# A cross-attention and FFN kernel: the out-projection four tiles ahead of the FFN in the last stage, and the residual loaded into the place of tiles 12 and 13

## The chip, the cores and the metric

The kernel runs on one core of a Trainium2 chip. The metric is the device time in microseconds (us) of one execution; lower is better. The engines are PE (TensorE, matrix products), DVE (VectorE), ACT (ScalarE), POOL (GpSimd) and SP (SyncE, which here only issues DMAs). Each works through its own list of instructions in order, and they meet through semaphores.

## The reference

Eight batch entries of 1024 tokens attend to 2048 context tokens each, with 16 heads of 32, and then pass through a linear layer whose input and weight are quantised in blocks of 32. Both halves add to the residual. Width is 512 throughout.

```python
def xattn(x, context, mask, Wq, Wk, Wv, Wo, bo, g1, b1, g2, b2):
    xn, cn = layer_norm(x, g1, b1), layer_norm(context, g2, b2)
    q, k, v = heads(xn @ Wq.T), heads(cn @ Wk.T), heads(cn @ Wv.T)
    scores = einsum('bqhs,bkhs->bhqk', q, k) / sqrt(32)
    attn = softmax(where(mask, scores, -inf))
    return einsum('bhqk,bkhs->bqhs', attn, v).reshape(B, Tx, C) @ Wo.T + bo

def ffn(x, weight, bias):            # both operands: blocks of 32, scale = max|block| / 7.5,
    xq, xs = mx_quantize(x)          # values rounded to the nearest of a 6-bit grid
    wq, ws = mx_quantize(weight)
    return (xq * xs) @ (wq * ws).T + bias

x = x + xattn(layernorm(x), ctx_1024, mask, ...)
x = x + ffn(layernorm(x), weight, bias)
```

## The kernel before

The kernel is written engine by engine: every engine has one block of code, an outer loop over the eight batch entries `b`, and the order of its instructions is the order in which the code is written. Nothing schedules them afterwards. A `wait_ge(semaphore, count)` holds everything behind it on the same engine.

**Stages of a batch.** `front()` turns and projects the tokens (queries, keys, values, in split half precision). Then eight units (`unit`, four head groups times two halves of the queries) make scores, exponentials and weighted sums in steps over 16 context tiles. Exponentials of a context tile lie in one of four buffers `PR[0]` to `PR[3]`, the four quarters of the big buffer `region` (`R`); POOL adds them in pairs (`pair`, L399) into `SUMS`, and DMAs that add on landing merge these (`merge`, L410). After the last unit comes the last stage, which the change is about.

**The last stage.** It works on 8 tiles of 128 tokens. For tile i:

- PE makes the out-projection, `contract(bank(i % 2), ...)` at L858 with `WO` (woT): four matmuls in float32 that the trace shows as eight passes. It waits for `s_x1`, that is for DVE to have emptied the bank two tiles before.
- POOL has added the bias `bo_all` to the residual `X1[:, i, :]` (`out_bias`, L456). `X1` lies in `R[:, 0:4096]`, the same memory as `PR[0]` and `PR[1]`.
- DVE adds bank and residual (`x1_tile`, L667), takes mean and variance (L498, L503, L510).
- POOL makes the inverse deviation (`x1_rstd`, L463, L465), and ACT writes the normalised tile to `XD` (L818).
- DVE quantises (`quantise`, L531 to L540), and POOL multiplies back to full size into `XD` (`full_size`, L470). POOL also adds the FFN bias `wb_all` to `X1` (L483).
- PE turns `XD` (four transposes, `turn`, L833) into bank 2 or 3, ACT copies it to `XDT` (L814), and PE makes the FFN contraction with `WD` (wdT) into bank 4 or 5 (again L858). `WD` doubles as `SUMS[4]` in the attention and is loaded again for each batch.
- DVE adds it to `X1` (`y_tile`, L685), and SP stores the tile.

On PE the step i of the loop is: out-projection i, turn i-2, FFN contraction i-2. DVE's step i is: quantise i-1, add i, FFN addition i-3, then a piece of the norm of the next batch's first tokens (`parts`, L498, L513). ACT's is: copy of turn i-2, normalise i. In the last two steps PE also turns the next batch's first tokens (`first_turns`, into banks 6 and 7), which ACT copies with an affine step (L718) and POOL subtracts (`low_tokens`, L380); the next batch's first projection pass (L864) waits for the last of these.

Bank 6 (`OB`) holds the weighted sums of a unit, bank 7 (`LB`) its row sums. Before the stage ACT copies bank 6 (L780), and in its first microsecond bank 7 (L760). DVE inverts the row sums (L601) and multiplies the outputs of the last unit (L608); out-projections 4 to 7 wait for that (`s_an`).

On SP the loads of the stage stand in this order behind the bias rows `bo` and `wb`: the FFN weights, the residual in two halves, the next batch's first tokens in two chunks, the projection weights. The first one waits for the last weighted step.

Of the kernel before, what the change touches and what calls it, by code (L numbers as in the profile page):

```python
# [8 lines left out]
P = 128  # L9
# [39 lines left out]
def build(nc, x, ctx_in, mask, wqT, wkT, wvT, woT, bo, affine_in, w, wb, out):  # L49
# [7 lines left out]
    KT = C // P  # L57
# [48 lines left out]
    with ExitStack() as es:  # L106
# [53 lines left out]
        PJB = [OB, LB]  # L160
        TURN = PS[0:J * QT, 4, 0:P]
# [77 lines left out]
        def _(e):  # L239
# [39 lines left out]
            for b in range(0, B):  # L279
# [45 lines left out]

                e.wait_ge(s_pv, b * (NU * KT) + NU * KT + 4)
                e.dma_start(SUMS[4], wd_dram).then_inc(s_fl, 16)
                for h in range(2):
                    e.dma_start(X1[:, 4 * h:4 * h + 4, :], xb[:, h]).then_inc(s_xl[h], 16)
# [163 lines left out]
        def _(e):  # L493
# [76 lines left out]
            for b in range(B):  # L570
# [93 lines left out]
                def x1_tile(i):  # L664
                    e.wait_ge(s_op, b * TT + i + 1)
                    e.wait_ge(s_xb, b * TT + i + 1)
                    e.tensor_tensor(X1[:, i, :], bank(i % 2), X1[:, i, :], ALU.add).then_inc(s_x1, 1)  # L667
# [162 lines left out]
        def _(e):  # L830
# [13 lines left out]
            for b in range(0, B):  # L844
# [212 lines left out]

                first_turns = turn_chunk(b + 1, 0, 6) if b + 1 < B else iter(())
                for i in range(TT + 2):
                    if i % 4 == 0 and i < TT:  # L1060
                        e.wait_ge(s_an, b * NU + NU + i // 4)
                    if i < TT:
                        if i >= 2:
                            e.wait_ge(s_x1, b * TT + i - 1)
                        contract(bank(i % 2), lambda cc: AO[:, ds((2 * cc + i // 4) * AO_UNIT + i % 4 * P, P)],
                                 lambda cc: WO[:, cc, :]).then_inc(s_op, 1)
                    if i >= 2:
                        k = i - 2
                        e.wait_ge(s_xd, 4 + b * TT + k + 1)
                        if k >= 2:  # L1070
                            e.wait_ge(s_tc, 4 + b * TT + k - 1)
                        turn(bank(2 + k % 2), lambda c: XD[k % 2][:, c * P:c * P + P]).then_inc(s_tt, 1)
                        if i >= TT:
                            next(first_turns, None)
                            next(first_turns, None)
                        e.wait_ge(s_tc, 4 + b * TT + k + 1)
                        if k >= 2:
                            e.wait_ge(s_y, b * TT + k - 1)
                        if k == 0:
                            e.wait_ge(s_fl, b * 16 + 16)  # L1080
                        contract(bank(4 + k % 2), lambda cc: XDT[k % 2][:, cc, :],
                                 lambda cc: WD[:, cc, :]).then_inc(s_ff, 1)
# [28 lines left out]
```

## Time and profile before

| | |
|---|---|
| median of 3 runs | 4893.51 us (4892.85 to 4898.69) |
| profiled execution, device time | 4894.66 us |
| its span, first to last instruction | 4892.9 us |
| PE busy | 4593.8 us |
| DVE, ACT, POOL busy | 3379.8, 2838.0, 2971.8 us |
| mean granted TensorE clock | 0.986 of full |

Busy time is the time in which an engine worked on an instruction; the rest of the span it waited. In a timeline each row is one instruction or a merged run of like ones; the number in brackets is how long its engine had been idle before it and what released it. Some rows further down cut the span in stretches; they give the stretch and its length, then for PE, PEld (weight loads), DVE, ACT and POOL the busy time and the number of instructions, then the granted TensorE clock (1.00 is 2.4 GHz, 0.50 is 1.2 GHz), the share of time in which the DMA engines were busy, and GB/s.

### The profile page before, as it was taken

The numbers are of one execution on the slowest core, as the hardware profiler recorded it, in microseconds if no ns is written. First come the engines' busy times: TensorE is split into PE (matmuls) and PEld (weight loads), VectorE is DVE, ScalarE is ACT, GpSimd is POOL, SyncE is SP. The second block draws the span as 40 slices with busy tenths as digits, with TensorE's granted clock in tenths as the row PEclk, the third lists the DMA queues.
The fourth block names the chain that finished last, engine by engine and source line by source line (L and its number), as shares of the span: only waits on it lengthen the run. The fifth ranks groups of instructions, "written<-read, shape, count | busy, mean of one in ns | idle before, by whom it ended". The sixth has DMA issues, their size and how long they took to land.

```text
span 4892.9 us, 65384 instructions
## 1 busy us (share of the span) xinstructions
PE 4593.8 (94%) x24720; PEld 1348.4 (28%) x24720; DVE 3379.8 (69%) x3943; ACT 2838.0 (58%) x5128; POOL 2971.8 (61%) x1818
## 2 busy tenths in 40 slices
PE   4999899998999989999899998999989999899998
PEld 2322242222422224222242222422224222342222
DVE  4788457884588855888357884588855887458873
ACT  3477634775347753477544774457744577446773
POOL 2278743777438773387634876347863578625875
PEclk9999999999999999999999999999999999999999
DMA  5255632555325553355533555335543355443552
GB/s 182 64 118 104 147 113 60 118 111 152 99 65 105 119 147 102 70 104 118 141 102 71 111 110 140 104 72 117 108 134 109 73 116 112 127 113 80 106 119 75
DMA packets 189918, 530.81 MB, mean 108 GB/s; under 512 B 28625, under 2 KB 102673, under 8 KB 148386
## 3 DMA queue, kind: packets, MB, share of 16 engines
q0 software_dynamic: 43776, 318.79, 32.3%
q1 hardware_dynamic: 145826, 207.83, 13.8%
q8 instruction: 195, 3.19, 0.3%
q14 instruction: 121, 0.99, 0.1%
HBM read 110.98 MB, written 21.01 MB: 27 GB/s over the span
## 4 chain that ended last, share of the span: by engine, by line
PE 75%; ACT 10%; DVE 6%; SPq 3%; DMA 3%; issue 2%; POOL 1%; ACTq 0%; DVEq 0%; POOLq 0%
PE banks L957 21%; PE banks L947 19%; PE banks L864 12%; PE banks L923 9%; PE banks L858 7%; ACT region L743 7%; PE banks L983 5%; DVE max_parts L583 3%; SPq L293 3%; PE banks L833 2%; DMA region<-in_x 1%; DVE region L574 1%; ACT values L814 1%; ACT region L718 0%; POOL wkT_wvT_wqT L399 0%
## 5 line engine op out<-in xcount | busy, mean ns | idle before, releaser
L583 DVE TENSOR_REDUCE max_parts<-banks 128x2 f32<-128x1024 f32 x2048 | 2400.1, 1218 | 469.2 <-PE banks L923 468.2
L743 ACT ACTIVATE region<-banks 128x512 f32<-128x512 f32 x4096 | 2211.0, 596 | 695.9 <-PE banks L947 656.9
L399 POOL TENSOR_TENSOR wkT_wvT_wqT<-region 128x1024 f32<-128x1024 f32 x608 | 1474.7, 2549 | 556.5 <-ACT region L743 554.3
L947 PE MATMUL banks<-queries_stacked,keys_stacked 98*128 98x512 f16 x4096 | 1298.4, 387 | 82.2 <-ACT region L743 50.7
L957 PE MATMUL banks<-region,values 128*32 128x512 f32 x8192 | 1100.6, 609 | 18.5 <-ACT region L743 7.7
L947 PEld LDWEIGHTS banks<-queries_stacked,keys_stacked 98*128 98x128 f16 x4096 | 289.0, 97 | 1438.7 <-ACT region L743 1356.4
L923 PE MATMUL banks<-keys_stacked,queries_stacked 33*128 33x512 f16 x4096 | 658.7, 384 | 7.0 <-DVE max_parts L583 3.5
L864 PE MATMUL banks<-region,wkT_wvT_wqT 128*128 128x512 f16 x2304 | 574.6, 388 | 48.1 <-POOL region L380 23.0
L601 DVE RECIPROCAL row_sums_inverse<-row_sums_inverse 128x128 f32<-128x128 f32 x256 | 232.0, 930 | 437.9 <-ACT row_sums_inverse L760 437.9
L399 POOL TENSOR_TENSOR sums<-region 128x1024 f32<-128x1024 f32 x160 | 395.7, 2631 | 25.7 <-ACT region L743 25.5
L574 DVE SCALAR_TENSOR_TENSOR region<-banks,region 128x512 f16<-128x512 f32 x192 | 132.2, 689 | 346.7 <-ACT region L726 345.7
L864 PE MATMUL banks<-wkT_wvT_wqT,region 128*128 128x512 f16 x1536 | 369.1, 380 | 0.0
L399 POOL TENSOR_TENSOR wdT<-region 128x1024 f32<-128x1024 f32 x128 | 314.4, 2595 | 1.5 <-ACT region L743 0.4
L923 PEld LDWEIGHTS banks<-keys_stacked,queries_stacked 33*128 33x128 f16 x4096 | 159.6, 93 | 559.9 <-issue 298.0
L726 ACT ACTIVATE region<-banks 128x512 f16<-128x512 f32 x192 | 113.7, 597 | 343.0 <-PE banks L864 286.2
L380 POOL TENSOR_TENSOR region<-row_sums_inverse,region 128x512 f16<-128x512 f32 x80 | 92.5, 1156 | 339.9 <-ACT region L718 339.9
L864 PEld LDWEIGHTS banks<-region,wkT_wvT_wqT 128*128 128x128 f16 x2304 | 214.6, 100 | 302.8 <-issue 65.0
L858 PE MATMUL banks<-wdT,values 128*128 128x512 f32 x512 | 249.8, 633 | 48.2 <-ACT values L814 48.2
L730 ACT ACTIVATE values<-banks 128x512 f32<-128x512 f32 x128 | 76.4, 597 | 334.0 <-PE banks L864 334.0
L858 PE MATMUL banks<-woT,queries_stacked 128*128 128x512 f32 x512 | 245.2, 627 | 26.3 <-DVE region L667 26.3
L416 POOL DMA_DIRECT2D wdT<-wkT_wvT_wqT x96 | 99.9, 1040 | 275.9 <-ACT region L743 155.3
L957 PEld LDWEIGHTS banks<-region,values 128*32 128x32 f32 x8192 | 161.6, 108 | 380.7 <-ACT region L743 219.3
(83 smaller groups left out, 2905.3 us busy)
## 6 DMA issues: line engine op xcount, KB each, us to landing
wdT<-wkT_wvT_wqT POOLq DMA_DIRECT2D x96, 1024.0 KB, 11.4
wkT_wvT_wqT<-wkT_wvT_wqT POOLq DMA_DIRECT2D x80, 1024.0 KB, 7.0
sums<-wkT_wvT_wqT POOLq DMA_DIRECT2D x72, 1024.0 KB, 7.0
keys_stacked<-region SPq DMA_DIRECT2D x768, 64.0 KB, 2.0
wkT_wvT_wqT<-sums POOLq DMA_DIRECT2D x40, 1024.0 KB, 7.0
region<-in_x SPq DMA_DIRECT2D x24, 1024.0 KB, 10.0
wkT_wvT_wqT<-weights_split SPq DMA_DIRECT2D x8, 3072.0 KB, 19.3
queries_stacked<-region SPq DMA_DIRECT2D x384, 64.0 KB, 2.0
```

The source lines that it names most:

```text
L293: e.dma_start(dst, KS[HD * j:HD * j + HD, part, gs, :]).then_inc(s_kd[h], 16)
L399: e.tensor_tensor(SUMS[dst][:, half], PR[i][:, half], PR[i + 1][:, half], ALU.add).then_inc(s_pr, 1)
L574: e.scalar_tensor_tensor(KS[:, 1, i, :], PJB[j % 2], 1.0 / W_SCALE, KS[:, 0, i, :], ALU.mult, ALU.subtract).then_inc(s_k2, 1)
L583: e.tensor_reduce(mpart[:, buf, :, a, t, c], MXB[parity], AX.X, ALU.max).then_inc(s_mxd, 1)
L601: inv = e.reciprocal(part, part)
L743: e.activation(PR[u % 4][:, j * HALF:j * HALF + HALF], score_bank(kt, j)[0], ACT.Exp, scale=SCALE).then_inc(s_ex, 1)
L858: mm = e.matmul(bank, lhs(cc), rhs(cc), start=(cc == 0), stop=(cc == CC - 1))
L864: mm = e.matmul(bank, lhs(p, cc), rhs(r, cc), start=(cc == 0 and i == 0), stop=(cc == CC - 1 and i == 2))
L923: mm = e.matmul(MXB[parity][:, i, :], QA[rows, ds(((2 * g + q) * J + 2 * a + i) * HALF + t * P, P)], KA[rows, ds((g * J + 2 * a + i) * C + ...
L947: e.matmul(dst, KA[0:STR, ds(ka + (j * C + (u + 1) * P), P)], QA[0:STR, ds(qa[j], HALF)], start=True, stop=True).then_inc(s_st, 1)
L957: mm = e.matmul(OB[HD * j:HD * j + HD, :], V[:, ds(v + u * D + HD * j, HD)], PR[u][:, j * HALF:j * HALF + HALF], start=False, stop=end, sk ...
L983: mm = e.matmul(LB[HD * j:HD * j + HD, :], ones[:, :], src[:, ds(j * HALF, HALF)], start=False, stop=closing and i == len(sums) - 1, skip_ ...
```

## The change

Three things are done. Line numbers of the changed kernel lie 3 to 6 above those before.

1. PE makes the out-projections of tiles 0 to 3 at once, in banks 0, 1, 6 and 7, and stays four tiles ahead: behind turn k (k below 4) comes out-projection k+4, then FFN contraction k. Tile 2 waits until ACT has copied bank 6, tile 3 until it has copied bank 7, later tiles for DVE's addition four tiles back.
2. From turn 4 on, turn k+1 is issued before FFN contraction k, so that ACT's copy of one turn runs while PE contracts another. The next batch's tokens are turned half before turn 7 and half before FFN contraction 7; since they are written to banks 6 and 7, the first half also waits for DVE's addition of tile 7.
3. SP loads the residual into `X1` before the FFN weights, as soon as the weighted step of context tile 13 of the last unit is done and POOL has added the last pair (context tiles 12 and 13, in `PR[0]` and `PR[1]`).

DVE, ACT and POOL keep their order; DVE only reads tile i from `out_bank(i)`.

```diff
+        LEAD = 4
+        out_bank = lambda i: bank((0, 1, 6, 7)[i % LEAD])
...
+                e.wait_ge(s_pv, b * (NU * KT) + (NU - 1) * KT + 14 + 4)
+                e.wait_ge(s_pr, 14 * (b * NU + NU) + 2)
+                for h in range(2):
+                    e.dma_start(X1[:, 4 * h:4 * h + 4, :], xb[:, h]).then_inc(s_xl[h], 16)
                 e.wait_ge(s_pv, b * (NU * KT) + NU * KT + 4)
                 e.dma_start(SUMS[4], wd_dram).then_inc(s_fl, 16)
-                for h in range(2):
-                    e.dma_start(X1[:, 4 * h:4 * h + 4, :], xb[:, h]).then_inc(s_xl[h], 16)
...
-                    e.tensor_tensor(X1[:, i, :], bank(i % 2), X1[:, i, :], ALU.add).then_inc(s_x1, 1)
+                    e.tensor_tensor(X1[:, i, :], out_bank(i), X1[:, i, :], ALU.add).then_inc(s_x1, 1)
...
+                def out_project(i):
+                    if i % 4 == 0:
+                        e.wait_ge(s_an, b * NU + NU + i // 4)
+                    if i == 2:
+                        e.wait_ge(s_oc, b * NU + NU + 1)
+                    if i == 3:
+                        e.wait_ge(s_on, b * NU + NU + 1)
+                    if i >= LEAD:
+                        e.wait_ge(s_x1, b * TT + i - LEAD + 1)
+                    contract(out_bank(i), ...).then_inc(s_op, 1)
...
-                for i in range(TT + 2):
-                    ...
+                for i in range(LEAD):
+                    out_project(i)
+                for k in range(TT):
+                    if k < LEAD:
+                        turn_quantised(k)
+                        out_project(k + LEAD)
+                    if k == TT - 2:
+                        e.wait_ge(s_x1, b * TT + TT)
+                        next(first_turns, None)
+                        next(first_turns, None)
+                    if LEAD - 1 <= k < TT - 1:
+                        turn_quantised(k + 1)
+                    if k == TT - 1:
+                        next(first_turns, None)
+                        next(first_turns, None)
+                    ffn(k)
```

`turn_quantised(k)` and `ffn(k)` are the old turn and FFN contraction with the waits they had.

PE at the start of the last stage of batch 0, as it was. `woT` rows are the out-projection, `ident,values` the turn of a quantised tile, `wdT` the FFN contraction; a row without x stands for one instruction:

```order
L858 MATMUL banks<-woT,queries_stacked 128x512 [waits unit_normalised]
L858 MATMUL banks<-woT,queries_stacked 128x512 x7
L858 MATMUL banks<-woT,queries_stacked 128x512 [waits x1_made]
L858 MATMUL banks<-woT,queries_stacked 128x512 x3
L833 MATMUL banks<-ident,values 128x128 [waits quantised]
L833 MATMUL banks<-ident,values 128x128 x3
L858 MATMUL banks<-wdT,values 128x512 [waits ffn_weights_loaded,quantised_copied]
L858 MATMUL banks<-wdT,values 128x512 x3
L858 MATMUL banks<-woT,queries_stacked 128x512 [waits x1_made]
L858 MATMUL banks<-woT,queries_stacked 128x512 x3
```

And as it is now:

```order
L864 MATMUL banks<-woT,queries_stacked 128x512 [waits unit_normalised]
L864 MATMUL banks<-woT,queries_stacked 128x512 x7
L864 MATMUL banks<-woT,queries_stacked 128x512 [waits unit_outputs_copied]
L864 MATMUL banks<-woT,queries_stacked 128x512 x3
L864 MATMUL banks<-woT,queries_stacked 128x512 [waits unit_row_sums_copied]
L864 MATMUL banks<-woT,queries_stacked 128x512 x3
L839 MATMUL banks<-ident,values 128x128 [waits quantised]
L839 MATMUL banks<-ident,values 128x128 x3
L864 MATMUL banks<-woT,queries_stacked 128x512 [waits x1_made,unit_normalised]
L864 MATMUL banks<-woT,queries_stacked 128x512 x3
L864 MATMUL banks<-wdT,values 128x512 [waits ffn_weights_loaded,quantised_copied]
L864 MATMUL banks<-wdT,values 128x512 x3
```

The wait for DVE's addition has gone from tile 2, which now waits for ACT's copy of bank 6; the out-projections of tiles 2, 3 and 4 have moved ahead of FFN contraction 0.

PE at the end of the same stage, where `ident,region` are the next batch's first tokens and `region,wkT_wvT_wqT` is its first projection. Before:

```order
L833 MATMUL banks<-ident,values 128x128 [waits quantised_copied,quantised]
L833 MATMUL banks<-ident,values 128x128 x3
L833 MATMUL banks<-ident,region 128x128 [waits tokens_normalised]
L833 MATMUL banks<-ident,region 128x128 x7
L858 MATMUL banks<-wdT,values 128x512 [waits y_made,quantised_copied]
L858 MATMUL banks<-wdT,values 128x512 x3
L833 MATMUL banks<-ident,values 128x128 [waits quantised_copied,quantised]
L833 MATMUL banks<-ident,values 128x128 x3
L833 MATMUL banks<-ident,region 128x128 [waits transposed_copied]
L833 MATMUL banks<-ident,region 128x128 x3
L833 MATMUL banks<-ident,region 128x128 [waits transposed_copied]
L833 MATMUL banks<-ident,region 128x128 x3
```

Now:

```order
L864 MATMUL banks<-wdT,values 128x512 [waits y_made,quantised_copied]
L864 MATMUL banks<-wdT,values 128x512 x3
L839 MATMUL banks<-ident,region 128x128 [waits tokens_normalised,x1_made]
L839 MATMUL banks<-ident,region 128x128 x7
L839 MATMUL banks<-ident,values 128x128 [waits quantised_copied,quantised]
L839 MATMUL banks<-ident,values 128x128 x3
L864 MATMUL banks<-wdT,values 128x512 [waits y_made,quantised_copied]
L864 MATMUL banks<-wdT,values 128x512 x3
L839 MATMUL banks<-ident,region 128x128 [waits transposed_copied]
L839 MATMUL banks<-ident,region 128x128 x3
L839 MATMUL banks<-ident,region 128x128 [waits transposed_copied]
L839 MATMUL banks<-ident,region 128x128 x3
```

FFN contraction 5 stands at the top of the second piece and turn 7 behind the first half of the token turns, where turn 6 stood ahead of them; the second half no longer stands behind turn 7.

SP behind the load of `bo`, before:

```order
L324 DMA values<-in_wb 128x512
L327 DMA wdT<-ffn_weights_quantised 128x2048 [waits pv_steps_done]
L329 DMA region<-in_x 128x4x512 x2
L243 DMA region<-in_x 128x4x512
L243 DMA values<-in_x 128x4x512
L275 DMA wkT_wvT_wqT<-weights_split 128x6144
```

Now:

```order
L327 DMA values<-in_wb 128x512
L333 DMA region<-in_x 128x4x512 [waits exponentials_paired,pv_steps_done]
L333 DMA region<-in_x 128x4x512
L335 DMA wdT<-ffn_weights_quantised 128x2048 [waits pv_steps_done]
L246 DMA region<-in_x 128x4x512
L246 DMA values<-in_x 128x4x512
```

The two halves of the residual moved ahead of the FFN weights, behind a wait of their own.

## Rows read from the trace of the kernel before

**Rows 1.** The page: busy time, share of the span and instructions of each engine.

```profile
PE 4593.8 (94%) x24720; PEld 1348.4 (28%) x24720; DVE 3379.8 (69%) x3943; ACT 2838.0 (58%) x5128; POOL 2971.8 (61%) x1818
```

**Rows 2.** Windows, the last stage of batches 0 and 7; columns as described above.

```profile
595.02:671.73 76.71, 66.10 (x181) 30.38 (x178) 53.05 (x119) 17.13 (x25) 42.80 (x46) 0.96 0.35 134
...
4811.18:4888.36 77.18, 64.58 (x164) 28.63 (x160) 42.32 (x93) 11.77 (x17) 34.52 (x40) 0.96 0.18 65
```

**Rows 3.** Timeline of PE, batch 0: start, duration, line, operation, tiles, [idle before].

```profile
595.02 7.13 PE L858 MATMUL banks<-woT,queries_stacked 128*128 128x512 f32 x16
605.51 5.40 PE L858 MATMUL banks<-woT,queries_stacked 128*128 128x512 f32 x8 [3.36 <-DVE region L667]
...
615.09 5.40 PE L858 MATMUL banks<-wdT,values 128*128 128x512 f32 x8 [2.40 <-ACT values L814]
...
625.05 3.70 PE L858 MATMUL banks<-wdT,values 128*128 128x512 f32 x8 [0.69 <-ACT values L814]
628.59 3.60 PE L858 MATMUL banks<-woT,queries_stacked 128*128 128x512 f32 x8
632.02 0.60 PE L833 MATMUL banks<-ident,values 128*128 128x128 f32 x4
...
666.88 1.04 PE L833 MATMUL banks<-ident,region 128*128 128x128 f32 x8
...
671.73 0.59 PE L864 MATMUL banks<-region,wkT_wvT_wqT 128*128 128x512 f16 x2 [0.29 <-POOL region L380]
```

**Rows 4.** Timeline of DVE, the same stage.

```profile
599.27 0.69 DVE L608 TENSOR_TENSOR queries_stacked<-queries_stacked,row_sums_inverse 128x512 f32<-128x512 f32 x1
604.77 0.69 DVE L667 TENSOR_TENSOR region<-banks,region 128x512 f32<-128x512 f32 x1 [4.81 <-POOL region L456]
...
610.17 0.69 DVE L540 TENSOR_TENSOR row_sums_inverse<-values,inv 128x512 fp8e4<-128x512 f32 x1
610.78 0.68 DVE L667 TENSOR_TENSOR region<-banks,region 128x512 f32<-128x512 f32 x1
...
624.15 0.68 DVE L667 TENSOR_TENSOR region<-banks,region 128x512 f32<-128x512 f32 x1
...
630.66 0.69 DVE L540 TENSOR_TENSOR row_sums_inverse<-values,inv 128x512 fp8e4<-128x512 f32 x1
...
648.73 0.69 DVE L667 TENSOR_TENSOR region<-banks,region 128x512 f32<-128x512 f32 x1 [1.48 <-PE banks L858]
...
655.03 0.69 DVE L540 TENSOR_TENSOR row_sums_inverse<-values,inv 128x512 fp8e4<-128x512 f32 x1
656.99 0.69 DVE L667 TENSOR_TENSOR region<-banks,region 128x512 f32<-128x512 f32 x1 [1.27 <-PE banks L858]
```

**Rows 5.** Timeline of POOL, the same stage.

```profile
603.40 2.48 POOL L456 TENSOR_TENSOR region<-region,values 128x512 f32<-128x512 f32 x2 [16.46 <-DMA region<-in_x]
...
610.94 1.04 POOL L470 TENSOR_TENSOR values<-row_sums_inverse,scale 128x512 f32<-128x512 fp8e4 x1 [1.99 <-DVE row_sums_inverse L540]
...
663.35 1.05 POOL L470 TENSOR_TENSOR values<-row_sums_inverse,scale 128x512 f32<-128x512 fp8e4 x1 [1.76 <-DVE row_sums_inverse L540]
```

**Rows 6.** Timelines of SP and POOL, the loads' landing at L329, the page's DMA issues.

```profile
595.15 0.33 SPq L327 DMA_DIRECT2D wdT<-ffn_weights_quantised  x1
...
581.99 4.95 POOL L399 TENSOR_TENSOR wkT_wvT_wqT<-region 128x1024 f32<-128x1024 f32 x2
...
DMA to landing us min/median/max: 7.6/8.8/10.5
...
sums<-wkT_wvT_wqT POOLq DMA_DIRECT2D x72, 1024.0 KB, 7.0
```

**Rows 7.** Windows: tile 2 of batch 0, then two periods from stage to stage.

```profile
605.51:610.91 5.40, 5.39 (x8) 2.03 (x8) 3.07 (x10) 0.81 (x1) 2.44 (x4) 0.68 1.09 413
...
1800.15:2400.84 600.69, 571.76 (x3093) 167.80 (x3089) 415.79 (x489) 353.59 (x640) 370.69 (x225) 0.99 0.47 108
2400.84:3006.25 605.41, 575.96 (x3093) 167.74 (x3089) 415.65 (x489) 353.38 (x640) 370.71 (x225) 0.98 0.46 108
```

More of the change, by code:

```diff
@@ L1055, in _ @@
                 unit(G - 1, 1, True)
-                first_turns = turn_chunk(b + 1, 0, 6) if b + 1 < B else iter(())
-                for i in range(TT + 2):
[L1060 to L1082, printed above, removed]
@@ new lines, in out_project @@
+                def out_project(i):
[7 more added lines that the diff above has]
+                        e.wait_ge(s_x1, b * TT + i - LEAD + 1)
+                    contract(out_bank(i), lambda cc: AO[:, ds((2 * cc + i // 4) * AO_UNIT + i % 4 * P, P)],
+                             lambda cc: WO[:, cc, :]).then_inc(s_op, 1)
@@ new lines, in turn_quantised, with ffn @@
+                def turn_quantised(k):
+                    e.wait_ge(s_xd, 4 + b * TT + k + 1)
+                    if k >= 2:
+                        e.wait_ge(s_tc, 4 + b * TT + k - 1)
+                    turn(bank(2 + k % 2), lambda c: XD[k % 2][:, c * P:c * P + P]).then_inc(s_tt, 1)
+                def ffn(k):
+                    e.wait_ge(s_tc, 4 + b * TT + k + 1)
+                    if k >= 2:
+                        e.wait_ge(s_y, b * TT + k - 1)
+                    if k == 0:
+                        e.wait_ge(s_fl, b * 16 + 16)
+                    contract(bank(4 + k % 2), lambda cc: XDT[k % 2][:, cc, :],
+                             lambda cc: WD[:, cc, :]).then_inc(s_ff, 1)
```

## Prediction

> **What bounds the kernel now.** I read the page first. PE is busy 94% of the span [rows 1], so a gain has to come from where PE waits or from its clock. The change touches one stage, the last of each of eight batches, so I cut the span by stage: from the first pass of the out-projection to the first projection pass of the next batch it takes 76.71 us in batch 0, with PE busy 66.10 us of it, and in the last batch, up to the end of DVE's last addition, 77.18 us [rows 2]. The other six stages repeat the first within 0.3 us. All times below count from that first pass (595.02 in batch 0).
>
> PE's timeline of the stage shows three parts [rows 3]. First two tiles in 7.13 us, then a wait of 3.36 us for DVE's addition on tile 0 (L667); tile 2 then takes 5.40 us where a later one takes 3.60, and the first FFN contraction, after another wait of 2.40 us, again 5.40. Then a regular loop: FFN contraction (3.70, with a wait of 0.69 before it for ACT's copy), out-projection (3.60), turn (0.60). From start to start the two contractions take 3.54 and 3.43, turn and wait 1.29: 8.26 us a tile. Last, a tail of FFN contractions and turns of the next batch's tokens, whose last one starts 4.85 us before the next batch's first pass (666.88 to 671.73).
>
> Why the first wait: the residual is loaded behind the FFN weights after the last weighted step (queue SP at 595.15), the 16 loads of it land after 7.6 to 10.5 us [rows 6], POOL adds the bias at 603.40 [rows 5], and DVE's first addition starts at 604.77 although DVE was through with the normalising product that starts at 599.27 [rows 4].
>
> The second chain that matters is the one across engines for a tile: DVE adds and takes statistics, POOL makes the deviation, ACT normalises, DVE quantises, and only then adds the next tile. Its rate where PE does not hold it is in [rows 4]: 6.01 us from tile 0 to 1, 13.37 us for the next two (6.69 each). After tile 3 the loop waits for PE, so I rebuild its own rate from DVE's quantising product (L540), behind which an addition can start after 0.61 us (the addition at 610.78 follows such a product at 610.17, and XD is written by POOL until 611.98, 1.20 us after the addition's start [rows 4, 5]). Tile 3 began at 624.15 and its product at 630.66: 7.12 us a tile; tile 4, which also has the next batch's centring in it, repeats that; tile 5, without it, repeats the 6.69; tile 6 runs from 648.73 to 655.03 plus 0.61: 6.91. This chain needs 6.0 to 7.1 us a tile and PE's loop 8.26, so PE's loop sets the pace now.
>
> **Part 1, the residual loaded earlier.** The two loads now stand ahead of the FFN weights, released by the weighted step of tile 13 and POOL's last pair, whose two halves start at 581.99 and take 4.95 us: about 586.95 [rows 6]. Landing is bounded by the present 7.6 to 10.5 us, with other loads on the same queue: 594.6 to 597.5, and sooner for the first half, which alone is wanted. POOL has nothing else then. The bias needs 1.24 us a tile, so tile 0 would be ready by 598.8 at the latest. Then DVE is late next: its product at 599.27 frees it 0.61 us later, so the first addition starts at 599.88, or 4.86, not 9.75. Price of the moved issues: SP waits there with nothing else behind it that is due before 595.15, and the last merge, which POOL issues before those two pairs (before 581.99) and which lands 7.0 us later, by 589.0, overlaps them by some 2 us; PE wants that buffer only in the last passes before 595.02, so about 5 us of slack cover it [rows 3, 6]. FFN weights and the next batch's tokens start no later than before, with 2 MB less ahead of the tokens. I take nothing for either.
>
> **Part 2, four tiles ahead.** PE does the out-projection of tiles 0 to 3 without a wait, 4 x 3.43 = 13.7. Banks 6 and 7 are free by then (ACT copied them before and at the start of the stage). The additions, at their own rate, start at 4.86, 10.9, 17.6, 24.2, 31.4, 38.5, 45.2 and 52.1 (6.01, 13.37 for two, 7.12 twice, 6.69, 6.91). XD of tile k is ready 1.20 us behind the start of addition k+1; for tile 7 it is (663.35 + 1.05) - 656.99 = 7.41 behind its own addition [rows 4, 5].
>
> **Part 3, copies beside contractions.** PE's loop is now turn 0.43, out-projection 3.43, FFN 3.43, the 0.6 us copy lying beside the out-projection: 7.29 instead of 8.26. Turn 0 at 13.7 (XD is ready at 12.1), then 21.0, 28.3, 35.6; out-projection 7 ends at 39.5, turn 4 follows at 39.7 when its XD comes, FFN 3 ends at 43.6. From here PE is ahead of the vector chain: turn 5 waits until 46.4 (2.8 us), turn 6 until 53.3 (3.1 us), FFN 5 and 0.9 us of the next batch's turns end at 58.1, turn 7 waits until 59.5 (1.4 us). Then FFN 6 to 63.4, the second half of the turns, FFN 7 to 67.7, and the next batch's first pass 4.85 after the turns' start: **68.2 instead of 76.7, 8.5 us a batch**. That end is set by ACT's and POOL's work on the last turned tokens and by FFN 7 at nearly the same time. DVE's additions of the output for tile k-3 stand where they stood, and each finds its FFN contraction done at least 2.9 us before, except the last two.
>
> The last batch has no centring and no next tokens: 4.86 + 6.01 + 5 x 6.69 + 6.01 = 50.3, turn 7 at 57.5, two contractions and the last addition: 65.7 instead of 77.2, 11.4 less.
>
> **Clock.** The granted clock was 0.68 over tile 2's 5.40 us, after PE had waited 3.36 us [rows 7]: at the lower level, 1.2 GHz, for most of them, against 3.70 for a contraction at 2.4 GHz. Both present falls are behind waits that go, and that is contained in the absolute times. But the new waits of 2.8 and 3.1 us are as long as the one of 2.40 that went with a fall. A fall on FFN 4 costs 1.7 us, which ends inside the 3.1 us wait; on FFN 5 it costs 0.3 after the 1.4 us wait; on FFN 6 it costs the whole 1.7. I allow 0.25 us a batch, 2 in all, and 8 x 1.7 = 13.6 at the most.
>
> This is where a page speaks against the change: the Trainium skill, "TensorE: Matmul & The Clock Gate", section "HAM oscillation — how this bites in real kernels", says that bursts parted by waits can each start at the low clock. Applied to all three new waits it gives the 13.6 us, 4836; the trace agrees that such falls exist and does not say which waits bring one.
>
> **Sum.** 7 x 8.5 + 11.4 = 70.9, less 2: 69 us. The profiled execution was 4894.66 (span 4892.9), the median of the runs shown is 4893.51; against the median the forecast is **4824.5 us** (-1.4%).
>
> **Rivals.** *A: the vector chain runs at its slow rate throughout.* With PE no longer apart from it, every tile could need the 7.12 us of tile 3: the last addition at 4.86 + 7 x 7.12 = 54.7, 2.6 later, and 4.4 later in the last batch. Gain 7 x 5.9 + 7.0 = 48: 4845. For it: POOL's and DVE's work touch in each tile. Against: tiles 1 and 2 ran at 6.69 with PE busy beside them. *B: the loads don't come earlier* (the queue or the wait holds them until about where they are). The lead stays and the chain starts at 9.75: 4.9 less in each stage, gain 7 x 3.6 + 6.5 = 32: 4862. Against it stand POOL's times in [rows 6]. *C, slower: the clock.* If after turn 5's wait PE stays at 1.2 GHz to the end of the stage, its 16.8 us of work there (4 contractions, 3 turns, 1.8 of next turns) take 33.6: 46.4 + 33.6 = 80.0, 3.3 more than now in seven batches and about 1 less in the last: 4916. It decides from about 13 us of that work at the low clock, since 4.5 us of new waits absorb some. For it: stretches elsewhere stay low long, and batches differ by 600.69 to 605.41 us for it [rows 7]. Against: here both falls ended inside one contraction and PE would be busy more than half of the time.
>
> **Numbers.** The forecast 0.80, A 0.11, B 0.04, C 0.03, nothing measurable 0.02. The seven periods from stage to stage spread by 4.7 us for clock stretches outside this stage; these may fall otherwise, some 11 us both ways. So the range goes from 70.9 + 11 less, 4811, to A's 4845 and, with a stretch more, 4846; it leaves out B, C and the chance of no effect. About 0.2% (10 us) is what a measurement of this kernel tells from no change: faster 0.95, same 0.02, slower 0.03.
>
> **What would show it.** In the changed trace: DVE's first addition near 4.9 us after the stage's start and not waiting for POOL; no PE wait before tile 2; PE's turns 0 to 3 at 7.3 us; waits for POOL's XD before turns 5, 6 and 7; stages of 68 us. Wrong would be an addition chain slower than 7 us a tile (A), a first addition at 9.7 (B), a PE wait before the last row sums, whose merge then landed late, or long stretches at the low clock (C).

## The result: 4819.44 us, 1.5% less, and the profile after

| | before | changed |
|---|---|---|
| median | 4894.36 us (4 runs) | 4819.44 us (4 runs, 4811.84 to 4827.74) |
| ratio | | 0.9846, 95% interval 0.9828 to 0.9864 |
| span of the profiled execution | 4892.9 us | 4810.0 us |
| the eight last stages together | 617.9 us | 546.1 us |
| everything else | 4275.0 us | 4264.0 us |

The forecast was 4824.5 us, in a range from 4811 to 4846. The last two rows come from the timelines of the two profiled executions: a stage runs from the first out-projection pass to the next batch's first projection pass (in the last batch to the end of the program).

The windows of the changed kernel, cut as in [rows 2] (stretch, length, busy time of PE, PEld, DVE, ACT and POOL, granted clock, DMA share, GB/s), for batches 0, 1, 2 and 7:

```profile
593.32:661.55 68.23, 61.29 (x181) 28.83 (x178) 52.62 (x119) 16.89 (x25) 40.66 (x45) 1.00 0.31 121
1186.84:1254.74 67.90, 61.29 (x180) 28.83 (x177) 52.54 (x119) 16.89 (x25) 40.42 (x45) 1.00 0.31 120
1778.42:1846.62 68.20, 63.04 (x181) 29.43 (x178) 52.56 (x119) 16.89 (x25) 41.29 (x45) 0.97 0.32 122
...
4740.07:4807.53 67.46, 61.03 (x164) 27.68 (x160) 41.87 (x93) 11.43 (x17) 32.12 (x39) 0.97 0.12 43
```

68.23 us stands where [rows 2] has 76.71, and 67.46 where it has 77.18. PE is busy 61.3 us of the stage instead of 66.1: of the difference, 3.6 us is that no contraction takes 5.40 us any more, as two did; the granted clock is 1.00 where it was 0.96.

PE's timeline of the stage in batch 0, to be held against [rows 3]:

```profile
593.32 14.00 PE L864 MATMUL banks<-woT,queries_stacked 128*128 128x512 f32 x32
607.15 0.60 PE L839 MATMUL banks<-ident,values 128*128 128x128 f32 x4
607.59 3.60 PE L864 MATMUL banks<-woT,queries_stacked 128*128 128x512 f32 x8
611.03 3.60 PE L864 MATMUL banks<-wdT,values 128*128 128x512 f32 x8
614.46 0.60 PE L839 MATMUL banks<-ident,values 128*128 128x128 f32 x4
...
629.51 3.60 PE L864 MATMUL banks<-woT,queries_stacked 128*128 128x512 f32 x8
633.06 0.66 PE L839 MATMUL banks<-ident,values 128*128 128x128 f32 x4
...
639.74 0.66 PE L839 MATMUL banks<-ident,values 128*128 128x128 f32 x4 [2.59 <-POOL values L476]
...
646.64 0.66 PE L839 MATMUL banks<-ident,values 128*128 128x128 f32 x4 [2.81 <-POOL values L476]
...
650.57 1.04 PE L839 MATMUL banks<-ident,region 128*128 128x128 f32 x8
652.82 0.66 PE L839 MATMUL banks<-ident,values 128*128 128x128 f32 x4 [1.22 <-POOL values L476]
...
656.75 1.04 PE L839 MATMUL banks<-ident,region 128*128 128x128 f32 x8
657.62 3.60 PE L864 MATMUL banks<-wdT,values 128*128 128x512 f32 x8
661.55 1.67 PE L870 MATMUL banks<-region,wkT_wvT_wqT 128*128 128x512 f16 x7 [0.33 <-POOL region L386]
```

Tiles 0 to 3 are one run of 14.00 us without a wait. Turns 0 and 1 start 7.31 us apart (8.26 before). Turn 4 at 633.06 follows the out-projection before it without a wait, and from there PE waits for POOL's product: 2.59, 2.81 and 1.22 us before turns 5, 6 and 7.

Where the first wait went is in the timelines of POOL, DVE and SP, against [rows 4 to 6], with the landing of the residual's loads (all 16):

```profile
591.15 2.51 POOL L462 TENSOR_TENSOR region<-region,values 128x512 f32<-128x512 f32 x2 [5.90 <-DMA region<-in_x]
```
```profile
597.57 0.69 DVE L614 TENSOR_TENSOR queries_stacked<-queries_stacked,row_sums_inverse 128x512 f32<-128x512 f32 x1
598.17 0.68 DVE L673 TENSOR_TENSOR region<-banks,region 128x512 f32<-128x512 f32 x1
```
```profile
585.35 2.60 SPq L333 DMA_DIRECT2D region<-in_x  x2
593.45 0.34 SPq L335 DMA_DIRECT2D wdT<-ffn_weights_quantised  x1
```
```profile
DMA to landing us min/median/max: 5.5/7.0/9.5
```

The loads are issued at 585.35, ahead of the FFN weights at 593.45, behind which they stood before, and POOL adds the first bias at 591.15. It waits 5.90 us for the load, but that wait ends two microseconds before the stage begins. DVE goes from its normalising product straight to the addition, 0.60 us later. The last merge, which now overlaps these loads, landed 6.96 to 9.23 us after its issue in the eight batches (6.95 to 9.23 before), and PE's waits ahead of the stage are the same 0.32 and 0.96 us.

### The profile page after: what moved, and what is told of

Same layout as the page of the kernel before. It is cut to its first block, busy times and chain, and to the rows that moved or that the text cites. A ratio compares the mean times of both kernels' runs of the same rounds, so it can differ in the third digit from the quotient of the medians.

```text
span 4810.0 us, 65399 instructions
## 1 busy us (share of the span) xinstructions
PE 4548.3 (95%) x24720; PEld 1337.8 (28%) x24720; DVE 3376.3 (70%) x3943; ACT 2835.9 (59%) x5128; POOL 2971.9 (62%) x1818
## 4 chain that ended last, share of the span: by engine, by line
PE 69%; DVE 11%; ACT 10%; issue 3%; SPq 3%; POOL 2%; DMA 1%; DVEq 0%; ACTq 0%; POOLq 0%
PE banks L963 21%; PE banks L953 19%; PE banks L870 12%; PE banks L929 9%; ACT region L749 8%; PE banks L989 5%; DVE max_parts L589 4%; SPq L296 2%; PE banks L839 2%; DVE amax L537 1%; DVE x_stats L504 1%; DVE region L673 1%; DVE qscale L539 1%; ACT values L824 1%; PE banks L864 1%
## 5 line engine op out<-in xcount | busy, mean ns | idle before, releaser
L386 POOL TENSOR_TENSOR region<-row_sums_inverse,region 128x512 f16<-128x512 f32 x80 | 92.4, 1155 | 339.9 <-ACT region L724 339.9
L824 ACT ACTIVATE values<-region,x_minus_mean_rstd,x_rstd 128x512 f32<-128x512 f32 x64 | 52.1, 814 | 341.6 <-POOL x_minus_mean_rstd L471 341.6
L864 PE MATMUL banks<-wdT,values 128*128 128x512 f32 x512 | 236.9, 607 | 0.0
## 6 DMA issues: line engine op xcount, KB each, us to landing
wdT<-wkT_wvT_wqT POOLq DMA_DIRECT2D x96, 1024.0 KB, 11.4
```

The source lines that it names most:

```text
L864: mm = e.matmul(bank, lhs(cc), rhs(cc), start=(cc == 0), stop=(cc == CC - 1))
```

## The experiments

Stage lengths below are those of batches 1 to 6 in each kernel's trace unless a batch is named; they repeat within 0.3 us where the clock does not fall.

### The load alone

```diff
# the kernel before, with the changed kernel's order of loads on SP only
+                e.wait_ge(s_pv, b * (NU * KT) + (NU - 1) * KT + 14 + 4)
+                e.wait_ge(s_pr, 14 * (b * NU + NU) + 2)
+                for h in range(2):
+                    e.dma_start(X1[:, 4 * h:4 * h + 4, :], xb[:, h]).then_inc(s_xl[h], 16)
                 e.wait_ge(s_pv, b * (NU * KT) + NU * KT + 4)
                 e.dma_start(SUMS[4], wd_dram).then_inc(s_fl, 16)
-                for h in range(2):
-                    e.dma_start(X1[:, 4 * h:4 * h + 4, :], xb[:, h]).then_inc(s_xl[h], 16)
```

> The kernel before with the early residual load alone; PE's order as before. Theory (two separate causes, the load gives the start of the chain, the lead gives the loop): DVE's first addition at 4.86 us after the stage's start instead of 9.75, tile 2 without a wait and at full clock, then the old loop of 8.26 us a tile: stage about 70.1 us (76.7 less the 6.5 by which PE's third tile moves), total about 4842 us. Rival (the load is worth only the 4.9 us by which the chain starts earlier, all the rest is the lead): 71.8 us a stage, about 4855. Rival (the lead does all, the load was hidden anyway): 76.7, 4894.

Measured: 4864.02 us, ratio 0.9942 [0.9925, 0.9958]; stages of 72.0 to 73.0 us. That is a miss for all three: the first addition came at 4.86 as expected, but the stage was 2.6 us longer than 70.1. PE's timeline, and the window over the contraction behind its two waits:

```profile
594.61 10.57 PE L860 MATMUL banks<-woT,queries_stacked 128*128 128x512 f32 x24
606.73 0.65 PE L835 MATMUL banks<-ident,values 128*128 128x128 f32 x4 [1.55 <-POOL values L472]
609.78 6.29 PE L860 MATMUL banks<-wdT,values 128*128 128x512 f32 x8 [2.39 <-ACT values L816]
615.91 3.60 PE L860 MATMUL banks<-woT,queries_stacked 128*128 128x512 f32 x8
```
```profile
609.78:615.91 6.13, 6.13 (x9) 2.55 (x9) 5.49 (x17) 0.80 (x1) 3.76 (x5) 0.57 0.30 128
```

There are two waits one after the other, 1.55 and 2.39 us, with 0.65 us of turns between them, and the contraction behind them takes 6.29 us at a granted clock of 0.57, mostly 1.2 GHz.

### The load alone, with PE kept at work

```diff
# the kernel of the load alone
+                def contract_some(bank):
+                    for cc in range(2):
+                        e.matmul(bank, AO[:, ds(2 * cc * AO_UNIT, P)], WO[:, cc, :], start=(cc == 0), stop=(cc == 1))
...
+                        if k == 0:
+                            contract_some(bank(4))
                         e.wait_ge(s_xd, 4 + b * TT + k + 1)
...
+                        if k == 0:
+                            contract_some(bank(5))
                         e.wait_ge(s_tc, 4 + b * TT + k + 1)
```

> The kernel of the early load alone, with two throwaway matmuls (a half contraction, 1.7 us at full clock, into a bank not in use) in each of its two PE waits, before turn 0 and before the first FFN contraction. Theory (the load alone fell short by the clock, which went down behind these two waits for 6.8 us): the low stretch goes, stages of 70 to 70.5 us instead of 72.7, total about 4843 instead of 4864. Rival (the shortfall is in the order, the clock only accompanies it): stages of 72.7 or more, 4864 or more.

Measured: 4840.35 us, ratio 0.9884 [0.9869, 0.9898]; stages of 70.1 to 70.4 us. PE does more work and the stage is 2.5 us shorter:

```profile
606.28 0.66 PE L835 MATMUL banks<-ident,values 128*128 128x128 f32 x4
606.77 1.88 PE L1062 MATMUL banks<-woT,queries_stacked 128*128 128x512 f32 x4
609.34 3.70 PE L860 MATMUL banks<-wdT,values 128*128 128x512 f32 x8 [0.68 <-ACT values L816]
```
```profile
594.15:625.00 30.85, 29.48 (x80) 13.22 (x76) 24.79 (x57) 4.93 (x7) 16.72 (x20) 1.00 0.57 221
```

The clock is 1.00 over the whole stretch, and the first FFN contraction takes 3.70 us. So the shortfall of the load alone was the clock, and without that fall the stage is 6.4 us shorter than before (6.5 computed). That figure includes the two falls of the kernel before, which are gone too.

### The lead alone

```diff
# the changed kernel, with the residual loaded behind the FFN weights again
-                e.wait_ge(s_pv, b * (NU * KT) + (NU - 1) * KT + 14 + 4)
-                e.wait_ge(s_pr, 14 * (b * NU + NU) + 2)
-                for h in range(2):
-                    e.dma_start(X1[:, 4 * h:4 * h + 4, :], xb[:, h]).then_inc(s_xl[h], 16)
                 e.wait_ge(s_pv, b * (NU * KT) + NU * KT + 4)
                 e.dma_start(SUMS[4], wd_dram).then_inc(s_fl, 16)
+                for h in range(2):
+                    e.dma_start(X1[:, 4 * h:4 * h + 4, :], xb[:, h]).then_inc(s_xl[h], 16)
```

> The changed kernel with the residual loaded where it was before (behind the FFN weights); four tiles ahead and copies beside contractions as changed. Theory: the first addition is back at 9.75 and every later one stands 4.9 us later than in the changed kernel, since the vector chain sets its end: stages of 73.0 us, total about 4861. Rival (the lead absorbs the late load): stages of 68 to 69, about 4822 to 4830.

Measured: 4855.72 us, ratio 0.9922 [0.9908, 0.9937]; stages of 72.4 to 73.4 us, 72.7 on average. DVE's timeline:

```profile
598.50 0.69 DVE L612 TENSOR_TENSOR queries_stacked<-queries_stacked,row_sums_inverse 128x512 f32<-128x512 f32 x1
603.97 0.69 DVE L671 TENSOR_TENSOR region<-banks,region 128x512 f32<-128x512 f32 x1 [4.78 <-POOL region L460]
```

The addition waits 4.78 us for POOL's bias again, and the stage ends 4.8 us later than in the changed kernel. The clock fell twice in batch 0 (contractions of 5.29 us behind waits of 2.99 and 2.59 us), and neither loss reached the end: the waits before turns 5 and 7 are 2.59 and 1.22 us, as in the changed kernel. The lead does not absorb a late load; the vector chain carries it to the end.

### No copies beside contractions

```diff
# the changed kernel
                 for k in range(TT):
                     if k < LEAD:
-                        turn_quantised(k)
                         out_project(k + LEAD)
                     if k == TT - 2:
                         e.wait_ge(s_x1, b * TT + TT)
-                        next(first_turns, None)
-                        next(first_turns, None)
-                    if LEAD - 1 <= k < TT - 1:
-                        turn_quantised(k + 1)
-                    if k == TT - 1:
+                    turn_quantised(k)
+                    if k >= TT - 2:
                         next(first_turns, None)
                         next(first_turns, None)
                     ffn(k)
```

> The changed kernel, with PE's order per tile out-projection k+4, turn k, FFN contraction k for all tiles: ACT's copy lies beside nothing, except beside the next tokens' turns for tiles 6 and 7. Theory (the vector chain sets the pace behind tile 3, so 0.7 us a tile on PE is not missed, and a contraction that is not behind a later tile's turn starts sooner): stages of 66.0 us against 68.0 of the changed kernel, total about 4806. Rival (the step from 8.26 to 7.29 us a tile is worth what it saves on PE): stages of 72 to 76 us, 4855 or more.

Measured: 4817.85 us, ratio 0.9835 [0.9821, 0.985]; stages of 67.11 us in six batches, 0.9 shorter than the changed kernel's 68.0. The direction was as expected, the size half of it: 66.0 us had been expected. PE's timeline of batch 0:

```profile
594.08 17.43 PE L864 MATMUL banks<-woT,queries_stacked 128*128 128x512 f32 x40
...
612.64 3.70 PE L864 MATMUL banks<-wdT,values 128*128 128x512 f32 x8 [0.69 <-ACT values L820]
...
655.42 0.60 PE L839 MATMUL banks<-ident,values 128*128 128x128 f32 x4
655.86 1.04 PE L839 MATMUL banks<-ident,region 128*128 128x128 f32 x8
656.73 3.68 PE L864 MATMUL banks<-wdT,values 128*128 128x512 f32 x8
661.55 1.67 PE L870 MATMUL banks<-region,wkT_wvT_wqT 128*128 128x512 f16 x7 [1.14 <-POOL region L386]
```
```profile
653.54 1.05 POOL L476 TENSOR_TENSOR values<-row_sums_inverse,scale 128x512 f32<-128x512 fp8e4 x1 [1.76 <-DVE row_sums_inverse L546]
654.54 1.45 POOL L489 TENSOR_TENSOR region<-region,values 128x512 f32<-128x512 f32 x1
655.95 2.45 POOL L386 TENSOR_TENSOR region<-values,region 128x512 f16<-128x512 f32 x2
```

The first six FFN contractions again have 0.69 us before them, the loop takes 8.26 us, and there is no other wait. The last contraction starts sooner than in the changed kernel (62.65 us after the stage's start instead of 64.30). PE then waits 1.14 us for POOL (0.78 in the later batches): its work on the next tokens (655.95, L386) had to queue behind its last product and bias (L476, L489), which hang on the vector chain. And that chain is late here, which the theory had not expected. Additions 6 and 7 start at 46.18 and 53.11, where the changed kernel has 45.16 and 52.06. ACT's timeline shows why:

```profile
636.76 0.60 ACT L820 ACTIVATE values<-banks 128x512 f32<-128x512 f32 x1 [6.96 <-PE banks L839]
637.25 0.80 ACT L824 ACTIVATE values<-region,x_minus_mean_rstd,x_rstd 128x512 f32<-128x512 f32 x1
```

ACT's order has the copy of turn 3 ahead of normalising tile 5. With the loop at 8.26 us turn 3 comes late, and tile 5 is normalised at 43.17 us after the stage's start instead of 41.43. So PE's slower loop did hold the vector chain, by 1.0 us.

### Turns behind contractions in the tail alone

```diff
# the changed kernel
-                    if k == TT - 2:
-                        e.wait_ge(s_x1, b * TT + TT)
-                        next(first_turns, None)
-                        next(first_turns, None)
-                    if LEAD - 1 <= k < TT - 1:
+                    if k > LEAD:
+                        turn_quantised(k)
+                    if k == LEAD - 1:
                         turn_quantised(k + 1)
-                    if k == TT - 1:
+                    if k == TT - 2:
+                        e.wait_ge(s_x1, b * TT + TT)
+                    if k >= TT - 2:
                         next(first_turns, None)
                         next(first_turns, None)
                     ffn(k)
```

> The changed kernel, but from tile 5 on PE turns a tile after the FFN contraction of the tile before, not ahead of it, and each half of the next tokens' turns lies between a turn and its contraction. Theory (the tail of the changed kernel loses time because ready contractions stand behind the wait for a late turn): the last FFN contraction starts earlier, stages of about 65.4 us, total about 4800. Rival (copies beside contractions are worth 0.7 us a tile in the tail too): stages 2 to 3 us longer than in the changed kernel, about 4840.

Measured: 4811.25 us, ratio 0.9831 [0.9816, 0.9846]; stages of 66.1 to 66.4 us, 1.8 shorter than the changed kernel's. The medians of this kernel, of the one before it and of the changed kernel cannot be told apart by their intervals; the stage lengths can. PE's last FFN contraction ended at 65.1 us, and the next batch's first pass came 1.3 us later, behind POOL once more. In this order PE does not stand before a late turn with a contraction ready behind it.

This kernel differs from the one before it in PE's order up to tile 4 alone: copies beside contractions there, none in the other. It keeps the additions of the changed kernel (45.15 and 52.05), and its stage is 1.0 us shorter than the 67.1 of no copies beside contractions. So the two halves of part 3 have opposite signs: 1.0 us gained in the loop, 1.8 us lost in the tail. In the profiled execution the eight stages take 529.7 us against 546.1 in the changed kernel, but the rest takes 4278.7 against 4264.0, and that hides the gain in the total.

### A shorter vector chain

```diff
# the changed kernel; DVE
-                    if 1 <= i <= TT:
-                        quantise(i - 1)
                     if i < TT:
                         x1_tile(i)
+                    if 1 <= i <= TT:
+                        quantise(i - 1)
# POOL
-                    if i > 0:
-                        full_size(i - 1)
                     if i < TT:
                         x1_rstd(i)
+                    if i > 0:
+                        full_size(i - 1)
```

> The changed kernel with one swap on DVE (the addition of tile i ahead of the quantising of tile i-1) and one on POOL (deviation of tile i ahead of the full-size product of i-1). Theory (the chain across DVE, POOL and ACT of 6.0 to 7.1 us a tile sets the pace behind tile 3): with two tiles in that chain at once the additions come 5.3 us apart or less until PE's 7.3 us hold them, the waits before turns 4 and 5 go, stages of about 64 us, total about 4790. Rival (DVE's or PE's own work sets the pace): stages within 1 us of the changed kernel's 68, about 4820.

Measured: 4807.96 us, ratio 0.9824 [0.9809, 0.9839]; stages of 66.5 to 68.0 us. In batch 0 addition 1 came 2.3 us behind addition 0, the next ones 5.2 to 6.8 us apart, and the last 8.3. Of the changed kernel's three waits those before turns 5 and 7 went (turn 4, which the expectation names, had none), but the stage gained only 1.4 us in five of the six batches. The gain ended at a wait on DVE, behind which PE stood before turn 6:

```profile
639.11 0.69 DVE L691 TENSOR_TENSOR region<-banks,region 128x512 f32<-128x512 f32 x1 [1.34 <-PE banks L864]
```
```profile
647.29 0.97 PE L839 MATMUL banks<-ident,values 128*128 128x128 f32 x4 [4.24 <-POOL values L476]
648.06 5.01 PE L864 MATMUL banks<-wdT,values 128*128 128x512 f32 x8
```

L691 is the addition of tile 3's FFN product. DVE stood before it for 1.34 us until PE had made that product, and a piece of the norm, the addition of tile 7 and the quantising of tile 6 stood behind it. PE waited 4.24 us for tile 6, and the clock fell behind that wait: 5.01 us for the contraction.

### The same, with the last addition one step later

```diff
# the kernel with the shorter vector chain; DVE
-                for i in range(TT + 3):
+                for i in range(TT + 4):
...
-                    if i >= 3:
-                        y_tile(i - 3)
+                    if i >= 4:
+                        y_tile(i - 4)
```

> The kernel with the swapped vector order, with DVE's last addition one step later (tile i-4 instead of i-3). Theory (with the faster chain DVE stood before the addition of tile 3's FFN product, which held the quantising of tile 6 and left PE 4.2 us idle before turn 6): that wait goes, stages of about 62.5 us instead of 66.6, total about 4778. Rival (DVE's or POOL's own work is the bound now): stages stay at 66, about 4808.

Measured: 4775.01 us, ratio 0.9754 [0.9734, 0.9775]; stages of 62.6 to 63.0 us. The wait before turn 6 shrank from 4.24 to 1.41 us, and with it went the fall of the clock, together the 4 us that the stage lost:

```profile
643.88 0.66 PE L839 MATMUL banks<-ident,values 128*128 128x128 f32 x4 [1.41 <-POOL values L476]
...
657.59 1.67 PE L870 MATMUL banks<-region,wkT_wvT_wqT 128*128 128x512 f16 x7 [0.33 <-POOL region L386]
```

### All orders together

```diff
# the kernel before this one; PE's tail as in the fifth experiment
+                    if k > LEAD:
+                        turn_quantised(k)
+                    if k == LEAD - 1:
+                        turn_quantised(k + 1)
                     if k == TT - 2:
                         e.wait_ge(s_x1, b * TT + TT)
-                        next(first_turns, None)
-                        next(first_turns, None)
-                    if LEAD - 1 <= k < TT - 1:
-                        turn_quantised(k + 1)
-                    if k == TT - 1:
+                    if k >= TT - 2:
                         next(first_turns, None)
                         next(first_turns, None)
                     ffn(k)
```

> The swapped vector order, the last addition one step later, and PE's tail with each turn behind the contraction of the tile before. If PE's work (about 60 us a stage) becomes the bound: stages of about 62 us, total about 4775. If the last turned tokens on ACT and POOL set the end: 63 to 64, about 4785, no better than the same with the changed kernel's tail.

Measured: 4773.43 us, ratio 0.9749 [0.9732, 0.9765]; stages of 62.3 to 62.6 us. That is 0.4 us a stage less on average than with the changed kernel's tail, and no difference in the medians. This is the fastest kernel of the study, some 46 us below the changed one. PE's own work here is 60.1 us by the contraction and turn times, so 2 us a stage are left to it.

## Why the prediction was right, and where it was not

**The start.** Computed: first addition at 4.86 us after the stage's start, loads landed by 594.6 to 597.5. Measured: 4.86, in seven of eight batches (5.13 in one), first half landed by 591.15. The bounds were taken from loads issued right behind the FFN weights; without those ahead they landed sooner (5.5 us at the least). Since DVE was the later one, that changed nothing. That the moved loads cost nothing elsewhere also held: PE has no wait ahead of the stage that it did not have before. The lead-alone kernel shows the price of this term: 4.8 us a stage, 4.9 computed.

**The chain.** Computed additions at 4.86, 10.9, 17.6, 24.2, 31.4, 38.5, 45.2 and 52.1. Measured in batch 0: 4.86, 10.86, 17.56, 24.24, 31.36, 38.48, 45.16, 52.06. The chain's own rate could be read from the trace of before although PE had held it from tile 3 on, because DVE's quantising product ends the chain of a tile whether or not PE lets it go on. This holds as long as PE's loop stays ahead of the chain: with the loop at 8.26 us (no copies beside contractions) additions 6 and 7 came 1.0 us later. In the other batches the last step took 6.57 instead of 6.91 us, which is where 67.9 instead of 68.2 comes from. Rival A, the slow rate for every tile, did not occur.

**The tail.** Computed 68.2 us, measured 67.9 to 68.2. The waits before turns 5, 6 and 7 were computed as 2.8, 3.1 and 1.4 and measured as 2.59, 2.81 and 1.22 in batch 0; the whole 7 x 8.5 + 11.4 = 70.9 us stands against 60.1 for the seven stages and 9.7 for the last, 69.8. The 617.9 - 546.1 = 71.8 of the table has 2.0 us more: it runs to the end of the program, and there the last store landed in 1.67 us where it had taken 3.67. Nothing in the change explains this, so it is luck: in the profiled executions of the other eight kernels it took 1.66 or 1.67 us in seven and 4.13 in the one without copies beside contractions.

**The last batch** was the one stage off its figure: 67.46 us against 65.7. Its last addition on the residual came at 50.26 (50.3 computed) and turn 7 at 57.54 (57.5). The fall of the clock lay on the last two contractions, where the text had said that it costs its full price. PE's timeline of its end, and the clock there:

```profile
4797.61 0.63 PE L839 MATMUL banks<-ident,values 128*128 128x128 f32 x4 [1.93 <-issue]
4798.07 8.73 PE L864 MATMUL banks<-wdT,values 128*128 128x512 f32 x16
```
```profile
4798.70:4802.10 3.40, 3.40 (x5) 1.33 (x4) 0.00 (x0) 0.22 (x1) 0.04 (x1) 0.50 0.02 5
```

Two contractions take 8.73 us instead of 7.03.

**The clock.** The allowance of 0.25 us a batch was about right (three more falls, one each in batches 2, 4 and 5), and so was the reason: a fall on FFN contraction 4 ends inside the next wait. In batch 2:

```profile
1825.14 0.65 PE L839 MATMUL banks<-ident,values 128*128 128x128 f32 x4 [2.60 <-POOL values L476]
1825.63 5.30 PE L864 MATMUL banks<-wdT,values 128*128 128x512 f32 x8
1831.70 0.66 PE L839 MATMUL banks<-ident,values 128*128 128x128 f32 x4 [0.77 <-POOL values L476]
```
```profile
1825.14:1828.56 3.42, 3.42 (x8) 1.78 (x9) 3.06 (x12) 1.30 (x2) 2.18 (x4) 0.58 0.20 77
```

The contraction takes 5.30 us at 0.58 of the clock, the wait before turn 6 is 0.77 us where batch 0 has 2.81, and the stage is as long as batch 0's. The Trainium skill ("TensorE: Matmul & The Clock Gate", section "HAM oscillation — how this bites in real kernels") shows a kernel in which every burst behind a wait of about 3 to 5 us starts at the low clock. Here the waits were 1.9 to 2.8 us, and the trace agrees with it for one burst in four of the eight stages, and only in the last did the fall cost time, about 1.7 us. The prediction weighed this at 13.6 us; by its own prices, falls behind all three waits would cost 0.3 + 1.7 us a batch, 16 us in all.

The prediction said that its absolute times contain the two falls of before. What it did not ask is which part of the change removes them: its rival B takes 4.9 us for the load and leaves the rest to the lead. The runs separate it, in us a stage (means of batches 1 to 6):

| | stage |
|---|---|
| before | 76.6 |
| load alone | 72.7 |
| load alone, PE kept at work | 70.2 |
| lead and copies beside contractions, without the load | 72.7 |
| load and lead, without copies beside contractions | 67.1 |
| load and lead, copies beside contractions in the loop alone | 66.1 |
| load and lead, changed kernel | 68.0 |

Taken in this order the load brings 3.9, the end of the falls another 2.5, the lead 3.1. Taken the other way round, the lead with its copies brings 3.9 and the load 4.8 on top: the shares depend on the order, and the load is worth the 4.9 us of rival B only once the lead is there.

**The step that was wrong is part 3.** It credited the copies beside contractions with PE's loop of 7.29 instead of 8.26 us. The loop did run at 7.3, and that is worth 1.0 us a stage, since it brings ACT's copy of turn 3 in time for the vector chain. But behind tile 3 that chain sets the pace, and turning ahead there cost 1.8 us a stage: PE stands before turn 7 with FFN contraction 6 ready behind it. Together part 3 lost 0.9 us. The time came out right all the same, because the prediction stepped through the order as it is, waits included. My own figures had that wait of 1.4 us and the contraction behind it side by side, and I did not ask what the other order would give. My remark that each output addition finds its contraction done at least 2.9 us before, except the last two, was also too wide: tile 5's found it done 0.8 us before. It cost nothing.

**Outside the stages** the range allowed 11 us both ways, and the profiled execution used all of it: 4264.0 us against 4275.0 before, with 46.5 us at the low clock outside the stages against 80.5. In the ten profiled executions of this study this part is 4264 and 4266 us where no stretch at the low clock is as long as 10 us, 4269 and 4273 with one, and 4273 to 4279 with two to four. What decides these stretches, which lie outside the stage that was changed, no run here settles. The same spread is in the changed kernel's four runs, 4811.84 to 4827.74; the 11.0 us by which the profiled execution gained outside the stages are of that kind. That the medians came within 5 us of the forecast is therefore in part luck; the stage lengths are not.

## What to carry to other kernels

In a loop across several engines, work out the rate of each chain by itself before crediting a saving to one: the product or copy that ends a tile's chain shows its rate even while something else holds it back. Here the prefetch was worth most where it started the slowest chain sooner and left PE no pair of waits behind which its clock fell; one contraction's worth of throwaway work spread over such a pair paid for itself (4864 to 4840 us). And on an engine that works in order, put what may come late behind what is ready, on DVE as much as on PE: moving one addition by a step was worth 33 us.

## What the runs showed of the hardware

A wait of 2.39 us behind one of 1.55 us, with 0.65 us of turns between, went with a granted clock of 0.57 over the next 6.13 us, and with PE kept at work in the two waits the clock stayed at 1.00; that fall made its contraction 2.7 us longer, where each of before had cost 1.8; waits of 2.59 and 2.81 us, 4 us of work apart, brought none in batch 0 of the changed kernel, and in batch 2 a wait of 2.60 at the same place of the program brought one. In the last batch one came behind waits of 1.88, 1.88 and 1.93 us. The residual's loads of 1 MB landed in 5.5 to 9.5 us when the FFN weights were not ahead of them on their queue, and in 7.6 to 10.5 us behind them [rows 6].

A small product of DVE in the vector chain, the scale of a tile, takes 0.17 us by itself and up to 1.11 us beside an addition of POOL. In the changed kernel, timelines of DVE and POOL:

```profile
629.41 1.11 DVE L539 TENSOR_SCALAR qscale<-amax 128x16 f32<-128x16 f32 x1
```
```profile
629.22 1.27 POOL L462 TENSOR_TENSOR region<-region,values 128x512 f32<-128x512 f32 x1
```

Of the 68 such products 41 take 0.6 us or more, and 40 of these end within 0.12 us of the end of POOL's bias addition (L462), in the kernel before as in the changed one. With the shorter vector chain only 4 of 68 are that long. No run shows what this alone is worth.
